# The residual of a gated MLP with LoRA: x from a PSUM transpose and a VectorE add, or accumulated by matmuls of x_hi and x_lo with the identity

## The reference

```
gate = x @ W_gate.T + 0.5 * (x @ A_gate[i].T) @ B_gate[i].T        # 512 -> 1376
up   = x @ W_up.T   + 0.5 * (x @ A_up[i].T)   @ B_up[i].T
act  = silu(gate) * up
down = act @ W_down.T + 0.5 * (act @ A_down[i].T) @ B_down[i].T    # 1376 -> 512
out  = x + down
```

## Time and profile before

| | us |
|---|---|
| median of three runs | 577.28 (576.72 to 578.58) |
| the profiled execution's own time | 577.4 |
| its span in the trace | 575.5 |
| PE busy in the span | 518.0 (90%) |
| PEld busy | 475.4 (83%) |
| DVE busy | 297.7 (52%) |
| ACT busy | 194.3 (34%) |
| POOL busy | 74.2 (13%) |

### The profile page before, as it was taken

The page is one execution under the profiler, slowest core; times in us unless marked ns, Lnnn a source line. Parts: engine busy times, 40 slices in busy tenths (PEclk is TensorE's granted clock), DMA queues, the critical chain, the costliest instruction groups (busy, mean ns, idle before and its releaser), DMA issues.

```text
span 575.5 us, 10131 instructions
## 1 busy us (share of the span) xinstructions
PE 518.0 (90%) x3169; PEld 475.4 (83%) x3169; DVE 297.7 (52%) x577; ACT 194.3 (34%) x394; POOL 74.2 (13%) x74
## 2 busy tenths in 40 slices
PE   0007897999999999999999999999999999999997
PEld 0006887798989898989999999999999999998987
DVE  7989768874444444444353535353535353535342
ACT  3613101743333333333333324242423333333331
POOL 7434412640000000000000000000000000000000
PEclk9999999899999999999999999999999999999999
DMA  7626898730404040404040403030303030303000
GB/s 286 235 55 203 288 324 291 180 103 23 113 5 115 2 119 0 120 0 119 0 115 5 114 6 110 10 110 10 107 13 107 13 107 13 107 13 107 14 19 19
DMA packets 32307, 53.20 MB, mean 92 GB/s; under 512 B 7586, under 2 KB 16194, under 8 KB 32290
## 3 DMA queue, kind: packets, MB, share of 16 engines
q1 hardware_dynamic: 32290, 53.00, 31.3%
HBM read 48.69 MB, written 4.28 MB: 92 GB/s over the span
## 4 chain that ended last, share of the span: by engine, by line
PE 85%; DVE 11%; DMA 1%; issue 1%; POOL 1%; ACT 0%; DVEq 0%; SPq 0%; ACTq 0%
PE ps_u L989 21%; PE ps_g L989 20%; PE ps_db L1025 12%; PE ps_da L1025 12%; PE ps_x L1016 3%; PE ps_x L967 2%; PE ps_u L937 2%; PE ps_g L999 2%; PE ps_g L1000 2%; PE ps_u L1000 2%; PE ps_u L999 2%; PE ps_g L937 2%; PE ps_x L1054 1%; DMA um<-xr 1%; PE ps_da L1083 1%
## 5 line engine op out<-in xcount | busy, mean ns | idle before, releaser
L825 DVE TENSOR_TENSOR b_spl<-b_raw,b_spl 64x512 fp32r<-64x512 f32 (+1 forms) x96 | 66.6, 695 | 52.5 <-ACT b_spl L499 49.0
L499 ACT CAST b_spl<-b_raw 64x512 fp32r<-64x512 f32 (+1 forms) x96 | 54.6, 569 | 76.8 <-PE ps_u L1000 76.8
L989 PE MATMUL ps_g<-w_hi,x_hi 128*128 128x512 f32 (+1 forms) x192 | 72.8, 379 | 0.0
L989 PE MATMUL ps_g<-w_lo,x_hi 128*128 128x512 f32 (+1 forms) x192 | 71.1, 370 | 0.0
L989 PE MATMUL ps_g<-w_hi,x_lo 128*128 128x512 f32 (+1 forms) x192 | 71.0, 370 | 0.0
L989 PE MATMUL ps_u<-w_lo,x_hi 128*128 128x512 f32 (+1 forms) x192 | 70.7, 368 | 0.0
L989 PE MATMUL ps_u<-w_hi,x_hi 128*128 128x512 f32 (+1 forms) x192 | 70.6, 368 | 0.0
L989 PE MATMUL ps_u<-w_hi,x_lo 128*128 128x512 f32 (+1 forms) x192 | 70.5, 367 | 0.0
L434 POOL COPY xt<-x 128x512 f32 (+1 forms) x15 | 9.8, 653 | 394.5 <-PE ps_x L1054 390.9
L861 DVE TENSOR_TENSOR h_act<-h_act,ps_u 128x512 f32<-128x512 f32 (+1 forms) x48 | 30.4, 633 | 52.2 <-PE ps_u L1000 52.1
L1025 PE MATMUL ps_da<-wd_hi,ht_hi 128*128 128x288 f32 (+1 forms) x176 | 54.6, 310 | 0.0
(11 more groups left out here) (167 smaller groups left out, 986.6 us busy)
## 6 DMA issues: line engine op xcount, KB each, us to landing
a_raw<-atab SPq DMA_DIRECT2D x64, 152.0 KB, 2.4
toep<-kpad SPq DMA_DIRECT2D x16, 512.0 KB, 5.4
b_raw<-btab SPq DMA_DIRECT2D x128, 64.0 KB, 2.1
stage<-wgu SPq DMA_DIRECT2D x8, 512.0 KB, 5.0
um<-xr SPq DMA_DIRECT2D x16, 256.0 KB, 5.7
x<-xT SPq DMA_DIRECT2D x8, 512.0 KB, 6.7
out<-y_sb SPq DMA_DIRECT2D x15, 256.0 KB, 2.1
b_raw<-btab SPq DMA_DIRECT2D x64, 44.0 KB, 1.8
```

What stands on the lines that cost most here:

```text
L499: nc.scalar.copy(b_spl[0:LR, up, 0:w], b_raw[slot][:, up * w:(up + 1) * w]).then_inc(b_hi, 1)
L825: V.tensor_tensor(b_spl[LR:P, up, 0:w], b_raw[slot][:, up * w:(up + 1) * w], b_spl[0:LR, up, 0:w].bitcast(F32), ALU.subtract).then_inc(b_l ...
L989: T.matmul(ps[:, 0:w], xs[:, q, kb, :], ws[:, kb, col:col + w], start=(kb == 0 and xs is x_hi and ws is w_hi), stop=False)
```

## The change

- The four transposes at line 1054, ACT's copy to `y_sb` at line 567, and the semaphores `res_ps` and `res_ok` with their waits on POOL, ACT, DVE and PE are removed.
- Behind `down_chunk(1)` and `lora_a(t+1)`, eight matmuls are added: `x_hi` and `x_lo`, four blocks each, as the loaded weights, and the 128 x 128 identity as the moving operand, each into 128 columns of `ps_da` or `ps_db`. The identity becomes a float32r tensor; the transposes read the same bytes as float32.
- `DA_W` becomes 256, so that two blocks fall into each accumulator. The down matmuls are then 256 columns for `ps_da` and 320 (256 + 64) for `ps_db`.
- `finish` becomes two copies of 256 columns from PSUM to `y_sb`. DVE now has the wait for the previous store.

```diff
-DA_W = 288
+DA_W = 256
...
-        ident = sb(top, "ident", [P, P])
+        ident_r = sb(top, "ident", [P, P], F32R)
+        ident = ident_r[:, :].bitcast(F32)
...
                     t = 2 * a + q + 1
-                    pool.wait_ge(res_ps, t)
                     pool.wait_ge(xlo_ok, t)
...
                 ht_hi_part(1)
-                act.wait_ge(res_ps, t + 1)
-                wait(act, y_out, 16 * t)
-                nc.scalar.copy(y_sb[:, :], ps_x[0][:, :]).then_inc(res_ok, 1)
                 if not last:
                     x_hi_part(na, nq, False)
...
                 dve.wait_ge(y_ps, t + 1)
-                dve.wait_ge(res_ok, t + 1)
-                V.tensor_tensor(y_sb[:, 0:DA_W], y_sb[:, 0:DA_W], ps_da[:, 0:DA_W], ALU.add).then_inc(y_ok, 1)
-                V.tensor_tensor(y_sb[:, DA_W:NL], y_sb[:, DA_W:NL], ps_db[:, 0:DB_W], ALU.add).then_inc(y_ok, 1)
+                wait(dve, y_out, 16 * t)
+                V.tensor_copy(y_sb[:, 0:DA_W], ps_da[:, 0:DA_W]).then_inc(y_ok, 1)
+                V.tensor_copy(y_sb[:, DA_W:NL], ps_db[:, 0:DB_W]).then_inc(y_ok, 1)
...
                 pe.wait_ge(xt_ok, t + 1)
-                wait(pe, res_ok, t)
...
                 pe.wait_ge(htlo_ok, (NC + 1) * t + 1)
-                for kb in range(KB):
-                    ins = T.transpose(ps_x[0][:, kb * P:(kb + 1) * P], xt[:, kb, :], ident[:, :])
-                ins.then_inc(res_ps, 1)
                 wait(pe, y_ok, 2 * t)
...
                 down_chunk(1)
                 if not last:
                     lora_a(t + 1)
+                for xs in (x_hi, x_lo):
+                    for kb in range(KB):
+                        ps = ps_da if kb < KB // 2 else ps_db
+                        col = kb % (KB // 2) * P
+                        T.matmul(ps[:, col:col + P], xs[:, q, kb, :], ident_r[:, :], start=False, stop=False,
+                                 skip_group_check=True)
                 pe.wait_ge(htlo_ok, (NC + 1) * (t + 1))
```

More of the change, by code:

```diff
@@ L175, in program @@
         ad_ps = sem("ad_ps")
-        res_ps, res_ok = sem("res_ps"), sem("res_ok")
         down_ps, td_ok, td_ps, tdhi_ok, tdlo_ok = (sem("down_ps"), sem("td_ok"), sem("td_ps"), sem("tdhi_ok"),
@@ L372, in _ @@
             nc.gpsimd.memset(half_pi[:, :], PI / 2).then_inc(consts, 1)
-            nc.gpsimd.memset(ident[:, :], 0.0).then_inc(ident_s, 1)
+            nc.gpsimd.memset(ident, 0.0).then_inc(ident_s, 1)
             pool.wait_ge(ident_s, 1)
-            nc.gpsimd.affine_select(out=ident[:, :], in_=ident[:, :], compare_op=ALU.not_equal, fill=1.0, base=0,
+            nc.gpsimd.affine_select(out=ident_r[:, :], in_=ident, compare_op=ALU.not_equal, fill=1.0, base=0,
                                     pattern=[[-1, P]], channel_multiplier=1).then_inc(ident_s, 1)
@@ L1016, in transpose_act @@
                         ins = T.transpose(ps_x[bank][0:rows, f * P:(f + 1) * P], h_act[:, s, f * P:f * P + rows],
-                                          ident[:, :])
+                                          ident)
                     ins.then_inc(ht_ps, 1)
@@ L1076, in transpose_td @@
                 pe.wait_ge(htlo_ok, (NC + 1) * (t + 1))
-                T.transpose(ps_x[1][:, 0:P], td_m[:, :, :].rearrange("p a r -> p (a r)"), ident[:, :]).then_inc(td_ps, 1)
+                T.transpose(ps_x[1][:, 0:P], td_m[:, :, :].rearrange("p a r -> p (a r)"), ident).then_inc(td_ps, 1)
             def down_lora(t):
```

## The result

| | before | changed |
|---|---|---|
| median of the runs, us | 577.93 (576.72 to 578.62, 4 runs) | 585.23 (583.86 to 586.25, 4 runs) |
| ratio, 95% interval | | 1.0127 (1.0096 to 1.0158) |
| profiled execution: own time, span | 577.4, 575.5 | 584.68, 582.8 |

The change makes the kernel 7.3 us slower. The forecast was 584.6 us with a span of 582.8.

The account below looks back on a forecast made before the run. PE, without a gap in the tile loop, was taken as the bound: 16 x (0.90 - 0.44) = 7.3 us on a median of 577.28 gave 584.6 us, with 582.6 to 586.4 as the range for 8 in 10.

Parts of the forecast that it names:

- PE's queue is the sum: In the tile loop PE never rests, so only PE's instructions count; a tile takes 29.2 us.
- The four transposes give 0.44 a tile: Removing four PE transposes per tile gains 0.44 us each tile, 7.0 us over 16 tiles.
- Eight times 0.112: The eight added PE matmuls cost 0.112 us each, their weight load as the floor: 0.90 us a tile.
- Rival B: Loads of the narrow matmuls hide; moving columns set the pace, 0.065 us each: 1.3 us in all, 578.6; chance 0.09.
- Rival C: Narrow float32r matmuls run as two passes with a load each: 1.78 us a tile, 598.7 us in all; chance 0.06.
- Rival D: A new wait on PE, or time falling differently over the clock's change: some 3 us either way; chance 0.05.
- The split costs nothing: Down matmuls of 256 and 320 columns for 288 each, and down_lora's four of 256: no change in sum.
- The other engines are in time: POOL's copy moves from 387.0 to about 382.5; ACT's and DVE's changed work and waits cost the span nothing.
- The end: The last output's two copies replace an add of 0.45 us and its 0.30 follow-up: 0, bounds -0.2 and +0.1.
- The sum: Over 16 tiles, 0.90 added less 0.44 removed on PE: 7.3 us slower.

Follow-up runs that it names:

- before256: The kernel before with only DA_W changed from 288 to 256 (down matmuls of 256 and 320 columns): 577.00 us, ratio to before 0.9979.
- no_res: The changed kernel without the eight added matmuls, the residual left out of the output: 569.87 us, ratio to the kernel before 0.9862.
- cols64: The changed kernel with the eight added matmuls streaming only 64 identity columns, same weight loads: 584.82 us, ratio to the kernel before 1.0105.
- interleave: The changed kernel with one of the eight narrow matmuls behind every three wide ones of down_chunk(1): 585.62 us, ratio to before 1.0118.

## Why the prediction was right

- **PE's queue is the sum.** Right. The loop had no wait before and has none after; the time moved by what PE's instructions cost. One reading was off: the granted clock is at 9 tenths from the ninth slice on, not from the eighth, which shows 8; from 100 to 106 us it was 0.50, the 1.2 GHz level. It lies ahead of the tiles that the periods compare.
- **The four transposes give 0.44 a tile.** Right: 0.427 by before256 and no_res.
- **Eight times 0.112.** Right in mechanism and size: the loads stand 0.112 apart, eight cost 0.914 a tile, four 0.467. cols64 shows that it is not the matmul's columns, which the trace of before could only suggest, and the 32-column loads of line 924 show that it is no fixed price per pair. Of the rows before, the load of 0.11 after PE had stood idle was the row that decided, and the 64-column matmuls of the convolution said the same of float32 weights. `lora_a` with its 0.89 alone could not have told load from streaming.
- **Rival B, loads that run ahead.** Refuted by cols64 and by interleave. The Trainium skill's 81 ns for a load and matmul pair at 128 columns (page "TensorE: Matmul & The Clock Gate", section "Back-to-back issue gap") is not met by float32r weights here: it is 0.112, and the measurement decides.
- **Rival C, two passes.** Refuted: eight records a tile and 0.11 each.
- **Rival D, a new wait.** None appeared in the lists of who PE waited for.
- **The split costs nothing.** Not quite: -0.053 us a tile in one pair of kernels and +0.051 in the other. A part of each is a slow piece of unknown cause that comes and goes with small changes, and the forecast had no term for that.
- **The other engines are in time.** Right: POOL's release by the DMA, 3.9 us earlier; DVE's added wait never ended a stall in the steady loop. The end takes 0.75 us before and after.
- **The sum.** 7.3 forecast; 7.3 by the spans (582.8 - 575.5), 6.9 by the periods. The prediction had 0.90 - 0.44 = 0.46 us a tile; measured are 0.914 - 0.427 - 0.053 = 0.434. The first two terms together came out 0.03 above that, at 0.487, and the unforeseen -0.053 takes that back and a little more. That the spans differ by just the 7.3 us of the sum is in part luck: the preparation, 0.2 us longer in the changed kernel, makes up for some of the term that was missing.

## What to carry to other kernels

Where PE has no gap, price an instruction by the larger of its columns and the load of the weights behind it: a 128 x 128 float32r matmul with 128 columns costs its 0.11 us of load in both places tried, and two of them (hi and lo) cost a little over twice the float32 transpose that they replace (0.914 against 0.427 for a tile's). Moving work from idle engines onto the full one was a loss here even though it deletes instructions, copies and semaphores elsewhere. The way to gain is the other way: take the work off PE, and then count the other engine's idle stretches one by one: the same 5.2 us of DVE work left the period as it was in one placement (29.17, and 3 us lost by the first tile and the preparation) and brought it to 28.71 in another, with a second `y_sb`, which made the kernel 5 us faster.

## What the runs showed that I had not expected

- A DVE transpose of 32 partitions x 128 elements takes 0.303 us and one starts every 0.33, longer than the 128-partition tensor op of 128 columns from PSUM (0.29); it can move blocks between partition groups while it transposes.
- In the interleaved order the cost of a narrow matmul shows in the chain at its wide neighbour (0.50 for 0.44, 0.41 for 0.36), so a line's own sum in the chain, 0.06, understates it by half.
